# Two matmul groups of a ViT layer's token MLP, each cut in half over neighbouring slots of TensorE's order

## The reference

```python
# token MLP, x: 16 images of 512 tokens x 256
gate = relu(x @ W0.T)            # 256 -> 512
up   = x @ W1.T                  # 256 -> 512
h    = (gate * up) @ Wo.T        # 512 -> 256
h    = concat([cls_tok, h])      # 513 rows
# attention, 16 heads of 16, with quantised ("bitlinear") projections
h = h + attention(layernorm(h))
# mixture of 8 experts, 2 per token
h = h + experts(layernorm(h), top_k=2)
```

## Time and profile before

| | |
|---|---|
| median of 3 runs | 2879.91 us (2872.59 to 2881.33) |
| span of the profiled execution | 2841.9 us |
| what lies around the span, median less span | 38.0 us |
| token phase, from the span's start to about | 2150 us |
| ten laps, each from slot 53 to the next lap's slot 53, 397.7 to 1675.6 us | 1277.9 us |
| busy in the span: PE, DVE, ACT, POOL | 80%, 55%, 43%, 30% |
| granted TensorE clock, mean of the span | 0.875 |

### The profile page before, as it was taken

The page is one execution under the profiler, slowest core; times in us unless marked ns, Lnnn a source line. Parts: engine busy times, 40 slices in busy tenths (PEclk is TensorE's granted clock), DMA queues, the critical chain, the costliest instruction groups (busy, mean ns, idle before and its releaser), DMA issues. The chain is left out here.

```text
span 2841.9 us, 46405 instructions
## 1 busy us (share of the span) xinstructions
PE 2261.1 (80%) x11984; PEld 1071.5 (38%) x11985; DVE 1574.0 (55%) x4115; ACT 1224.3 (43%) x2360; POOL 838.6 (30%) x750
## 2 busy tenths in 40 slices
PE   3798878687787878686787878778713999999998
PEld 2333333333332332333232333322211666666665
DVE  4576757575575657566565657667326333333333
ACT  1254545443454534444443535445404444444443
POOL 2212223131322213131312213131213555555554
PEclk9798989897888989788878989889756999999999
DMA  2222122121212222121211122122023333333332
GB/s 84 71 64 71 53 79 68 46 61 48 69 53 61 54 72 67 46 61 55 62 54 53 56 74 63 38 71 57 23 81 127 57 55 56 53 54 54 54 54 42
DMA packets 181075, 172.01 MB, mean 61 GB/s; under 512 B 40002, under 2 KB 169620, under 8 KB 180884
## 3 DMA queue, kind: packets, MB, share of 16 engines
q1 hardware_dynamic: 150612, 134.94, 16.3%
q0 software_dynamic: 30272, 34.80, 7.7%
HBM read 100.82 MB, written 68.93 MB: 60 GB/s over the span
## 5 line engine op out<-in xcount | busy, mean ns | idle before, releaser
L1101 DVE TENSOR_REDUCE mxs<-bank 128x1 f32<-128x512 f32 x1024 | 684.3, 685 | 561.0 <-PE bank L489 525.0
L793 ACT ACTIVATE pt<-bank 128x512 f32<-128x512 f32 x1024 | 589.6, 596 | 697.1 <-PE bank L498 689.5
L489 PE MATMUL bank<-ks,qs 96*128 96x512 bf16 x1024 | 436.7, 428 | 115.1 <-DVE mxs L1101 104.3
L498 PE MATMUL bank<-qs,ks 99*128 99x512 bf16 x1024 | 433.9, 425 | 7.2 <-ACT pt L793 6.9
L507 PE MATMUL bank<-pt,v_sb 128*32 128x512 f32 x2048 | 328.3, 719 | 0.0
L1627 POOL DMA_INDIRECT out<-y_sb,ids x136 | 215.5, 1585 | 267.8 <-DMA out<-y_sb,ids 206.1
L489 PEld LDWEIGHTS bank<-ks,qs 96*128 96x128 bf16 x1024 | 106.2, 104 | 499.0 <-DVE mxs L1101 344.3
L1673 PE MATMUL bank<-gu_h,xh 128*128 x544 | 208.2, 383 | 10.3 <-issue 7.4
L1756 DVE TENSOR_TENSOR hl<-bank,hh 128x512 bf16<-128x512 f32 x136 | 94.0, 691 | 209.5 <-ACT hh L1726 209.5
L1752 DVE TENSOR_TENSOR hid_e<-bank,act_g 128x512 f32<-128x512 f32 x136 | 94.0, 691 | 208.3 <-PE bank L1673 208.3
L1673 PE MATMUL bank<-gu_h,xl 128*128 x544 | 206.9, 380 | 0.0
(11 more groups left out here) (276 smaller groups left out, 3477.3 us busy)
## 6 DMA issues: line engine op xcount, KB each, us to landing
qs<-qk_dram SPq DMA_DIRECT2D x128, 128.0 KB, 2.4
ks<-qk_dram SPq DMA_DIRECT2D x64, 192.0 KB, 3.0
xt<-x_t SPq DMA_DIRECT2D x16, 512.0 KB, 3.9
h_dram<-h_sb SPq DMA_DIRECT2D x16, 512.0 KB, 3.6
qs<-qk_dram SPq DMA_DIRECT2D x128, 64.0 KB, 2.1
ks<-qk_dram SPq DMA_DIRECT2D x64, 128.0 KB, 2.9
hw<-h_dram SPq DMA_DIRECT2D x16, 512.0 KB, 5.2
out<-hw SPq DMA_DIRECT2D x16, 512.0 KB, 2.9
```

What stands on the lines that cost most here:

```text
L489: mm(score[u % 2][:, :], qs[0:QK, h, blk(t)], ks[0:QK, h, :], start=True, stop=True) \
L498: mm(scoret[u % 2][:, :], ks[0:QK + MROWS, h, blk(t)], qs[0:QK + MROWS, h, :], start=True, stop=True).then_inc(s("pe_st"), 1)
L793: f(pt[:, t % 2, j, :], scoret[u % 2][:, :], ACT.Exp).then_inc(s("act_exp"), 1)
L1101: v.reduce_max(mxs[:, t, g * GH + j:g * GH + j + 1], score[u % 2][:, :], AX.X).then_inc(s("dve_mx"), 1)
```

## The change

The two matmuls of each gate and up block now stand in two neighbouring slots: gate blocks in slots 28/29, 32/33, 36/37 and 40/41, up blocks in 30/31, 34/35, 38/39 and 42/43. The first matmul carries the wait, the second the signal. The output projection's four tiles stand in slots 0, 1, 4 and 5, one each. What consumes them moves along: the ReLU to the slot of the second half (29, 33, 37, 41), the product to 32, 36, 40 and 44 (before: 32, 35, 39, 43), the copies to `h_sb` to slots 2 and 6. No instruction is added or taken away.

```diff
-GATE_AT = (28, 33, 36, 40)
+GATE_AT = (28, 32, 36, 40)
 UP_AT = (30, 34, 38, 42)
-HIDDEN_AT = (32, 35, 39, 43)
+HIDDEN_AT = (32, 36, 40, 44)
+OUT_AT = (0, 1, 4, 5)
...
-                    if T.ok and at in UP_AT:
-                        e = UP_AT.index(at)
-                        wait(pe, s("dve_hid"), EC, T, e)
-                        for c in range(DC):
-                            last = mm(d1[:, :], w1[:, c, blk(e)], xt[:, T.par, c, :], start=(c == 0), stop=(c == DC - 1))
-                        last.then_inc(s("pe_up"), 1)
-                    if P.ok and at in (0, 4):
-                        k = at // 4
-                        if k == 0:
+                    if T.ok and at - at % 2 in UP_AT:
+                        e, c = UP_AT.index(at - at % 2), at % 2
+                        if c == 0:
+                            wait(pe, s("dve_hid"), EC, T, e)
+                            mm(d1[:, :], w1[:, c, blk(e)], xt[:, T.par, c, :], start=True, stop=False)
+                        else:
+                            mm(d1[:, :], w1[:, c, blk(e)], xt[:, T.par, c, :], start=False, stop=True) \
+                                .then_inc(s("pe_up"), 1)
+                    if P.ok and at in OUT_AT:
+                        t = OUT_AT.index(at)
+                        k = t // 2
+                        if t == 0:
                             wait(pe, s("dve_hid"), EC, P, EC)
                             if X.ok:
                                 wait(pe, s("dve_h2"), TB, X, TB)
-                        elif X.ok:
+                        if t == 2 and X.ok:
                             wait(pe, s("act_x2t"), DC, X, DC)
-                        for t in (2 * k, 2 * k + 1):
-                            for e in range(EC):
-                                last = mm((d0, d1)[k][:, D * (t % 2):D * (t % 2 + 1)], hid[:, e, blk(t)], wo[:, e, :],
-                                          start=(e == 0), stop=(e == EC - 1))
-                        last.then_inc(s("pe_h"), 1)
+                        for e in range(EC):
+                            last = mm((d0, d1)[k][:, D * (t % 2):D * (t % 2 + 1)], hid[:, e, blk(t)], wo[:, e, :],
+                                      start=(e == 0), stop=(e == EC - 1))
+                        if t % 2:
+                            last.then_inc(s("pe_h"), 1)
...
-                    if T.ok and at in GATE_AT:
-                        e = GATE_AT.index(at)
+                    if T.ok and at - 1 in GATE_AT:
+                        e = GATE_AT.index(at - 1)
                         wait(act, s("pe_gate"), EC, T, e + 1)
...
-                    if P.ok and at in (1, 5):
+                    if P.ok and at in (2, 6):
                         k = at // 4
                         wait(act, s("pe_h"), 2, P, k + 1)
```

More of the change, by code:

```diff
@@ L525, in body @@
                         pv(*st, u // 4 - 1)
-                    if T.ok and at in GATE_AT:
-                        e = GATE_AT.index(at)
-                        if e == 0:
+                    if T.ok and at - at % 2 in GATE_AT:
+                        e, c = GATE_AT.index(at - at % 2), at % 2
+                        if e == 0 and c == 0:
                             pe.wait_ge(s(f"x_in{T.par}"), T.half * 16 + 16)
@@ L531, in body @@
                                 wait(pe, s("dve_fk"), DC, P, DC)
-                        wait(pe, s("act_relu"), EC, T, e)
-                        for c in range(DC):
-                            last = mm(d0[:, :], w0[:, c, blk(e)], xt[:, T.par, c, :], start=(c == 0), stop=(c == DC - 1))
-                        last.then_inc(s("pe_gate"), 1)
-                    if T.ok and at in UP_AT:
-                        e = UP_AT.index(at)
-                        wait(pe, s("dve_hid"), EC, T, e)
-                        for c in range(DC):
-                            last = mm(d1[:, :], w1[:, c, blk(e)], xt[:, T.par, c, :], start=(c == 0), stop=(c == DC - 1))
-                        last.then_inc(s("pe_up"), 1)
-                    if P.ok and at in (0, 4):
-                        k = at // 4
-                        if k == 0:
+                        if c == 0:
+                            wait(pe, s("act_relu"), EC, T, e)
+                            mm(d0[:, :], w0[:, c, blk(e)], xt[:, T.par, c, :], start=True, stop=False)
+                        else:
+                            mm(d0[:, :], w0[:, c, blk(e)], xt[:, T.par, c, :], start=False, stop=True) \
+                                .then_inc(s("pe_gate"), 1)
+                    if T.ok and at - at % 2 in UP_AT:
+                        e, c = UP_AT.index(at - at % 2), at % 2
+                        if c == 0:
+                            wait(pe, s("dve_hid"), EC, T, e)
+                            mm(d1[:, :], w1[:, c, blk(e)], xt[:, T.par, c, :], start=True, stop=False)
+                        else:
+                            mm(d1[:, :], w1[:, c, blk(e)], xt[:, T.par, c, :], start=False, stop=True) \
[4 more added lines that the diff above has]
+                        if t == 0:
                             wait(pe, s("dve_hid"), EC, P, EC)
```

## The result

| | kernel before | changed kernel |
| --- | --- | --- |
| median us, 20 runs each, same chip | 2873.34 (2865.5 to 2881.33) | 2881.86 (2875.11 to 2891.42) |
| ratio, 95% interval | | 1.0027 (1.0016 to 1.0038) |
| profiled execution: span, PEclk | 2841.9, 0.88 | 2881.0, 0.87 |

The loss is about 8 us and clear of the uncertainty, though just inside the 0.3% that I had counted as no change; slower had a chance of 0.13. Two more pairs of measurements on other chips gave 1.0011 (1.0001 to 1.0021) and 1.0002 (0.9992 to 1.0013), and a third 1.0007 (0.9990 to 1.0024): the change costs between nothing and 0.3%.

What follows compares the result with a forecast made beforehand. PE was taken to set a lap's pace except where it waits, with part of its length due to 1.2 GHz. Slot 39's 5.2 us and the clock's 7 us took 12.2 off 2879.9, giving 2867.7, say 2868 us; range 2852 to 2886.

Steps and rivals of the forecast that it cites:

- Gate and up blocks: PE, slots 28 to 43: eight more boundaries per lap, each costing 0, upper bound 0.1 us each.
- The wait in slot 39: PE's 0.40 us wait before L641 goes in laps 1 to 13, gaining 5.2 us; bounds 0 to 5.2.
- The clock: Shorter laps redraw the sequence of clock changes: 7 us gained over ten laps, bounds -38 to +41 us.
- What lies around it: Time outside the profiled span, 38.0 us by the median, taken as unchanged.
- The chain from slot 44: DVE's last product moves ahead of L1313 in slot 44 and just fits: cost 0, bounds 0 to 0.60 us per lap.
- The third rival: DVE's product delays the chain from slot 44 by up to 7.8 us, giving 2882.5 us; chance 0.06.
- The output projection: Halving it in slots 0 and 4 and moving its copies gains 0, at most 3.9 us, and costs 0.
- The first, no net change: Only slot 39's 5.2 us is won, clock sequence the same on average: 2874.7 us, counted as no change; chance 0.34.
- The second: Clock rival: three more long laps in ten cost 16 us, less 5.2, giving 2891 us; chance 0.12.

Runs made afterwards that it cites:

- e13: Kernel before, unchanged, run again on a slower chip: 2873.21 us, ratio 0.9999.
- e14: Changed kernel, unchanged, run again on a slower chip: 2878.20 us, ratio 1.0007 against the kernel before.
- e2: Changed kernel, unchanged, profiled once more on a faster chip: 2856.37 us, ratio 1.0011 against the kernel before.
- e8: Kernel before with up block 2 whole in slot 39 ahead of the PV group, its product in slot 40, nothing in halves: 2836.35 us, ratio 0.9954.
- e1: Kernel before, unchanged, profiled once more on a faster chip: 2853.64 us, ratio 1.0000.
- e9: Changed kernel with every second up half ahead of its PV group, slot 35's too: 2837.98 us, ratio 0.9939 against the kernel before.
- e11: Same kernel as e8, measured again on another chip: 2832.62 us, ratio 0.9929 against the kernel before.
- e7: Changed kernel with three second up halves ahead of their PV groups, slot 35's left behind: 2842.76 us, ratio 0.9968 against the kernel before.
- e18: e8 with the eight list transfers issued from slot 40 instead of 34: 2897.05 us, ratio 1.0086 against the kernel before.

## Why the prediction was wrong, step by step

**Gate and up blocks, "each costs nothing": wrong, and this is the step that failed.** For a half between score matmuls it held: 0.86 us, as the earlier trace rows give. But I read the price of one kind of boundary and used it for eight. The halves of slots 31, 35, 39 and 43 stand behind a PV group, and there each costs 0.10 us, my upper bound, because its weights are not loaded ahead; in slot 39 the way back to 32 columns costs 0.09 more. Together 0.5 us a lap, 6 us in 13 laps, where I had 0. Which groups stand next to each other, and that their form changes (128*32 beside 128*128), was in the earlier trace rows.

On a chip with the hold, as the one of the result, the loss is made up otherwise. What stands ahead of the hold's end is waited for in any case, so neither the gain in slot 39 nor the price of the pieces ahead of it counts; the 0.6 us of product 2, which now stands behind it, does: 0.56 us in 12 laps by e13 and e14, 6.7 of the 8.5 us measured, though e14's ratio by itself shows no loss. The prediction has no such wait, and the trace that it reads has none either.

**The wait in slot 39: right, and undersized.** It goes: idle before the line was 6.9 us in 16 times, and is 1.8 in 3 in e2. Up to L545 it was worth 0.46 us, the idle row and its edges, and 0.58 against the 0.88 us that the PV group takes to L641 in e8; my bound of 0.40 was the idle row alone, which starts at the end of the longer matmul record. The net of both steps is +0.05 us a lap where I had -0.40.

**The clock, -7 us: unfounded.** It was called a choice and not a reading, and it was to follow from a shorter lap; the lap is not shorter. Ten laps of e1 and e2 differ by 1.3 us. The kernels whose laps are shorter (e8, e9, e11) did gain more than their rows of slots 28 to 44 give, so the idea may have something, but no run gives it a price.

**"What lies around it, 38.0 us": wrong.** In every run with a profile about 1.8 us lie around the span, not a few tens. The rest is a comparison of unlike things. The median of three runs was 6.6 us above that of twenty (2873.34). The chips with the hold take about 20 us more than those without, and the profile of before has no hold, while its times are those of a chip with it (that these runs had it is argued from their times; they have no profile). The other 10 us are the profiled execution's own luck: 2841.9 us is among the shortest of the kernel on any chip. I argued from a profile and a time that did not belong to the same conditions, and 38 us unexplained, beside a forecast gain of 12, should have stopped me.

**The chain from slot 44: right.** DVE in slot 44 of the lap shown, answering to the earlier trace rows:

```profile
1021.45 0.69 DVE L1107 TENSOR_REDUCE mxs<-bank 128x1 f32<-128x512 f32 x1 [1.78 <-PE bank L490]
...
1022.05 0.68 DVE L1237 TENSOR_TENSOR hid<-bank,relu 128x512 f32<-128x512 f32 x1
...
1022.65 0.16 DVE L1319 RECIPROCAL rc<-bank 4x4 f32<-4x4 f32 x1
```

L1319 starts 1.20 us after the maximum, as forecast, and PE's wait in slot 53 is 147.1 us in 16 times in e2 against 147.9 in e1. The third rival, a product that delays DVE, did come true on the chips with the hold, but for product 2 in slot 40.

**The output projection: right as far as it can be told.** The matmul behind ACT's `x_t` still waits 0.30 us. In the lap shown the second copy to `h_sb` starts at 954.25 and DVE reads it at 957.97, 3.1 us after it ends, where 3.4 were forecast. The wait in slot 12 is no longer either (24.5 us in 16 times in e2, 24.3 in e1).

**The rivals.** The first, no net change, is nearest, for a reason that it did not name: the gain of slot 39 came and was paid back next to it. The second did not come on a chip without the hold: no more long laps in e2 (four of ten over 131 us) than in e1 (four).

## What to carry over

Where matmul groups of different column widths alternate, count the changes of width before cutting or moving a group: a f32 block behind a narrow group costs 0.10 us here, and two narrow groups side by side save 0.12. Moving one whole block to the other side of the narrow group brought 0.5 to 0.7% on chips without the hold, of which the rows explain 0.27%, and nothing on one with it; halving eight blocks brought nothing on either. And when the profiled execution and the timed runs differ by more than the effect, find out what is in between, with a second profile, before forecasting.

## What the runs showed of the hardware

- A PV group (128*32) starts 0.09 us later behind full-width matmuls (0.31 us for 0.22 behind a score, 0.95 for 0.86 behind a half). It takes 1.00 us if a full-width matmul follows and 0.88 if L641's group of the same width does (e8). A f32 half or block of 128 columns behind it takes 0.10 us more than behind a score, its weights not being loaded ahead (e7). All of these are the same in every lap.
- In three of the six measurements, each on its chip, eight indirect transfers of GpSimd in a row keep late completions of PE from DVE and ACT until 11.5 to 12.7 us after the first one (means of 11.9 to 12.3), while PE goes on starting matmuls. Completions due up to 5 us after it are on time (slots 40 to 42 in e18), some due at 7 us are late already. It costs about 20 us of 2873, and four transfers do not show it.
